# Sixteen column-tiled products in the output projection, expert weights loaded later, one loop of ScalarE written out

## What is computed

```python
q, k, v = heads(ln(x) @ Wq.T + bq), heads(ln(x) @ Wk.T + bk), heads(ln(x) @ Wv.T + bv)
out = softmax(q @ k.T / sqrt(8)) * head_mask @ v        # per head
x = x + merge(out) @ Wo.T + bo                          # the output projection
y = ln(x)
shared = gelu(y @ Wfc_s + bfc_s) @ Wproj_s + bproj_s
topk_p, topk_i = top_k(softmax(y @ Wr), 2)              # renormalised to gates
routed = sum over the 2 chosen e of gate[e] * (gelu(y @ Wfc[e] + bfc[e]) @ Wproj[e] + bproj[e])
x = x + shared + routed
```

## Time and profile before

| | us |
|---|---|
| time, median of 3 runs | 620.09 (620.05 to 621.78) |
| the profiled execution, its own time | 626.37 |
| its span, first to last instruction | 624.5 |
| outside of the span | 1.87 |

### The profile page before, as it was taken

One profiled execution on the slowest core, in us unless ns is written; L12 is line 12 of the kernel. 1 busy time (PEld: TensorE's weight loads), 2 busy tenths in 40 slices (PEclk: granted clock), 3 DMA queues, 4 the chain that ended last, 5 costly groups with the idle time before them and its releaser, 6 DMA issues. The chain is left out here.

```text
span 624.5 us, 21597 instructions
## 1 busy us (share of the span) xinstructions
PE 604.4 (97%) x8090; PEld 393.9 (63%) x8090; DVE 496.0 (79%) x1076; ACT 449.0 (72%) x971; POOL 279.3 (45%) x477
## 2 busy tenths in 40 slices
PE   6888899999999999999999999999999999999997
PEld 3443557665455555545555455457799999989966
DVE  7799789999899899899899889636466666666557
ACT  4976788888888888888878878884255555555551
POOL 6856520132542543542542632656545554545510
PEclk8998989999999999999999999999999999999999
DMA  6795954211312322223223221002222222222173
GB/s 172 214 306 175 268 155 112 66 53 43 95 50 63 83 55 66 74 54 77 64 57 80 59 58 43 20 27 67 62 64 66 64 67 60 67 59 68 47 264 149
DMA packets 43836, 57.63 MB, mean 92 GB/s; under 512 B 11130, under 2 KB 31482, under 8 KB 43754
## 3 DMA queue, kind: packets, MB, share of 16 engines
q1 hardware_dynamic: 39434, 47.59, 26.9%
q0 software_dynamic: 4320, 8.89, 4.3%
HBM read 35.76 MB, written 20.42 MB: 90 GB/s over the span
## 5 line engine op out<-in xcount | busy, mean ns | idle before, releaser
L979 DVE TENSOR_REDUCE mx<-ps 128x2 f32<-128x1024 f32 x256 | 306.5, 1214 | 32.0 <-PE ps L1400 27.3
L837 ACT ACTIVATE probs<-ps 128x512 f32<-128x512 f32 x512 | 292.8, 602 | 46.2 <-PE ps L1428 31.4
L1428 PE MATMUL ps<-q_op,k_op 128*32 128x512 bf16 x2048 | 201.9, 383 | 3.3 <-DMA q_op<-mxT 2.1
L1400 PE MATMUL ps<-k_op,q_op 96*32 96x512 bf16 x2048 | 160.4, 383 | 3.6 <-DVE mx L979 3.2
L1443 PE MATMUL ps<-probs,v_op 128*32 128x256 f32 x2048 | 158.5, 380 | 0.2 <-ACT probs L837 0.2
L895 ACT ACTIVATE probs<-ps,b_cur 128x128 f32<-128x128 f32 x284 | 80.9, 368 | 65.3 <-PE ps L1643 60.6
L711 POOL DMA_INDIRECT results<-rest,row_id x71 | 73.0, 1028 | 75.1 <-DVE rest L1282 58.0
L1400 PEld LDWEIGHTS ps<-k_op,q_op 96*32 96x32 bf16 x2048 | 56.9, 97 | 63.1 <-DVE mx L979 21.1
L1428 PEld LDWEIGHTS ps<-q_op,k_op 128*32 128x32 bf16 x2048 | 59.8, 96 | 57.7 <-ACT probs L837 10.0
L1443 PEld LDWEIGHTS ps<-probs,v_op 128*32 128x32 f32 x2048 | 66.1, 109 | 41.6 <-issue 1.4
L604 POOL DMA_INDIRECT slots<-route_sb,slot_u x64 | 63.5, 992 | 54.4 <-ACT probs L837 45.7
(11 more groups left out here) (176 smaller groups left out, 555.7 us busy)
## 6 DMA issues: line engine op xcount, KB each, us to landing
q_op<-q_scr SPq DMA_DIRECT2D x96, 96.0 KB
k_op<-k_scr SPq DMA_DIRECT2D x96, 96.0 KB
w_sb<-in_W SPq DMA_DIRECT2D x18, 256.0 KB, 4.6
probs<-slots SPq DMA_DIRECT2D x71, 64.5 KB
q_scr<-probs SPq DMA_DIRECT2D x8, 384.0 KB, 3.3
k_scr<-probs SPq DMA_DIRECT2D x8, 384.0 KB, 3.0
k_scr<-probs SPq DMA_DIRECT2D x8, 256.0 KB, 3.8
probs<-results SPq DMA_DIRECT2D x4, 512.0 KB, 6.2
```

Source lines behind the costliest of these rows:

```text
L837: nc.scalar.activation(probs[:, i, j, :], ps[:, BANK["key", b, hg, s], :], ACT.Exp, scale=float(D) ** -0.5).then_inc(s_exp, 1)
L979: nc.vector.reduce_max(mx[:, slot % 2, 2 * p:2 * p + 2], ps[:, bank:bank + 2, :], AX.X).then_inc(s_max, 1)
L1400: last = nc.tensor.matmul(ps[c, BK_A + a % 4, :], q_op[hg][0:SH, j, P * i + c.start:P * i + c.stop], k_op[hg][0:SH, j, :], start=True, sto ...
L1428: last = nc.tensor.matmul(ps[c, bank, :], k_op[hg][:, j, P * i + c.start:P * i + c.stop], q_op[hg][:, j, :], start=True, stop=True)
```

## The change

Three edits:

- `project_out` (new L1463) makes each of its four products of 128 rows of the output as four column-tiled ones with 32 rows each: sixteen, of the same K = 128 and the same 128 streamed columns, into the same places of PSUM. It holds for all 8 sequences, the last of which is projected between the `up`s.
- `load_experts` is split. The biases go out with group 1 of sequence 0 and `fill_slots` with group 2. The weights of one expert (512 KB) go out with each group of the sequences 1 and 2 and with the first group of sequence 3.
- ACT's loop over tiles 8 to 63 is written out, with constants in its waits.

```diff
--- before.py
+++ after.py
@@ -388,14 +388,15 @@
                 to = slots[E * REGION:E * REGION + E * TR, :].rearrange("(e p) c -> p e c", p=P)
                 sp.dma_start(to, y2s[1].rearrange("p n k c -> p (n k) c")).then_inc(s_fill, 16)
 
-            def load_experts(hg):
-
-                if hg == 0:
-                    sp.dma_start(b2_sb[:, :, :], b2.partition_broadcast(P)).then_inc(s_b2, 16)
-                    sp.dma_start(b1_sb[:, :, :], b1).then_inc(s_wffn, 16)
-                for e in range(hg, NE, HG):
-                    sp.dma_start(w1_sb[:, e, :], W1[:, e, :]).then_inc(s_wffn, 16)
-                    sp.dma_start(w2_sb[:, e, :, :], W2[:, e, :, :]).then_inc(s_wffn, 16)
+            def load_biases():
+
+                sp.dma_start(b2_sb[:, :, :], b2.partition_broadcast(P)).then_inc(s_b2, 16)
+                sp.dma_start(b1_sb[:, :, :], b1).then_inc(s_wffn, 16)
+
+            def load_expert(e):
+
+                sp.dma_start(w1_sb[:, e, :], W1[:, e, :]).then_inc(s_wffn, 16)
+                sp.dma_start(w2_sb[:, e, :, :], W2[:, e, :, :]).then_inc(s_wffn, 16)
 
             def feed(b):
                 first, last = isinstance(b, int) and b == 0, isinstance(b, int) and b == B - 1
@@ -408,10 +409,12 @@
                         load_shift(b, hg + 1)
                     elif not last:
                         load_shift(b + 1, 0)
-                    if first:
-                        load_experts(hg)
-                        if hg == 1:
-                            fill_slots()
+                    if first and hg == 1:
+                        load_biases()
+                    elif first and hg == 2:
+                        fill_slots()
+                    elif not first and (b - 1) * HG + hg < NE:
+                        load_expert((b - 1) * HG + hg)
 
             sequences(feed)
 
@@ -897,10 +900,7 @@
 
             for u in range(RING):
                 tile_gelus(u, u % TQ)
-            with act.Fori(1, TILES // RING) as it:
-                for u in range(RING):
-                    tile_gelus(it * RING + u, u % TQ)
-            for t in range(TILES // RING * RING, TILES):
+            for t in range(RING, TILES):
                 tile_gelus(t, t % TQ)
 
 
@@ -1459,7 +1459,9 @@
                 pe.wait_ge(s_o, b + 1)
                 bank = wait_for_bank("project", b) if b < B - 1 else BK_M
                 for i in range(NT):
-                    last = nc.tensor.matmul(ps[:, bank, C * i:C * (i + 1)], o_sb[:, P * i:P * (i + 1)], wo_sb[:, :], start=True, stop=True)
+                    for c in QUARTERS:
+                        last = nc.tensor.matmul(ps[c, bank, C * i:C * (i + 1)], o_sb[:, P * i + c.start:P * i + c.stop], wo_sb[:, :],
+                                                start=True, stop=True)
                 last.then_inc(s_ap, 1)
 
             def transpose_y(b):
```

## The result

Seven executions of the kernel after took 626.36 to 628.72 us, median 627.93. Beside the seven of the kernel before that belong to them (620.05 to 624.73, median 623.18; the first three are those shown ahead) the ratio is 1.007, 95% interval 1.0039 to 1.010. The forecast was 614.2 us, faster, with a range up to 618.8. The profiled execution took 628.69 us with a span of 626.9, against 626.37 and 624.5 before: it is 2.4 us longer, where the sum said 5.9 us shorter. So 8.3 us are to be found.

What follows compares the result with a forecast made beforehand. PE was taken to set the pace in the attention with next to no slack. From the 620.09 us median, -3.9 (weights), -2.1 (seven projections), +0.1 (eighth) and 0 (ACT's loop) gave 614.2 us, range 611.0 to 618.8.

Steps and rivals of the forecast that it cites:

- the sum: Whole kernel: -3.9 for later weights, -2.1 for seven projections, +0.1 for the eighth, -5.9 us in all.
- What bounds the kernel: Attention: PE sets the pace with next to no slack, 10.4 us of products per group of heads.
- Edit 1, -3.9: Sequence 0, shift rows issued at 69.92: later weights remove PE's stall behind queued transfers, -3.9 us (bounds 0 to -4.0).
- stall moves: Rival, sequences 1 to 3: groups now carrying weights stall PE, 3.9 us each, 625.9 us with three; chance 0.08.
- stall stays: Rival, sequence 0: the group load alone makes the shift rows late, only the projection's gain is left, 618.1 us; chance 0.12.
- Edit 2, 7 x 0.30: Seven projections in the attention: sixteen column-tiled products avoid the tiling switches, 0.30 us saved each, -2.1 us.
- The eighth, +0.1: Last projection, between whole-array products: it gets the tiling switches; entry hidden by a wait, exit costs 0.1 to 0.15 us.
- Edit 3, 0: Tile stage: ACT's loop ends lie inside time it would spend waiting for PE, so 0 (bounds -2.4 to +2.0 us).
- The signs: Even shift rows, no wait for them, full clock, 1.55 to 1.6 us around a projection, tile stage unchanged without new ACT waits.
- R2: Rival theory of the experiments: later weights delay something in sequences 1 to 3, taking the gain back, 1.000 or above; no chance given.

Runs made afterwards that it cites:

- e2: Kernel before with the projection's sixteen column-tiled products for four as the only edit; 1.0005 of the kernel before.
- q4: Kernel before with ACT's tile loop written out as the only edit; 1.0003 of the kernel before.
- g1: Kernel before, unchanged, run again for a second profile; no ratio given, it is the kernel before of its set.
- e1: Kernel before with only the later loads (weights, biases, fill), the projection as four products; 0.9972 of the kernel before.
- p4: The same kernel as e1, run once more in a later set; 0.9959 of the kernel before.
- g2: Kernel after, unchanged, run again; 1.0066 of the kernel before.
- q2: Kernel after with a POOL memset of 64 columns and a wait for it ahead of the first put of sequences 2 to 7; 1.006 of the kernel before.
- g4: Kernel after with sixteen products in sequences 0 to 2 alone, four in the others; 0.9977 of the kernel before.
- p2: Kernel after with a POOL memset of 192 columns between the waits and the first put of sequences 2 to 7; 0.9969 of the kernel before.
- e4: Kernel after with a POOL memset of 4 columns ahead of each sequence's first put; 0.9963 of the kernel before.
- q3: As q2, with the last projection as four products; 1.0016 of the kernel before.
- r2: As q3, with a memset of 256 columns in place of 64; 1.0029 of the kernel before.
- e3: Kernel before with a POOL memset of 4 columns ahead of each sequence's first put; 1.0012 of the kernel before.

## Why the prediction was wrong, point by point

**What bounds the kernel** held: PE sets the pace. Without held posts what the products saved came out of the distance from the first to the seventh projection in full.

**Edit 1, -3.9**: the mechanism was right, the size was read from one execution that had the stall at its largest. PE's wait for the shift rows in the second profile of before and in two others with the early weights (e2, q4):

```profile
77.35 0.40 PE L1428 MATMUL ps<-q_op,k_op 128*32 128x512 bf16 x4 [2.20 <-DMA q_op<-mxT]
```

```profile
75.44 0.40 PE L1428 MATMUL ps<-q_op,k_op 128*32 128x512 bf16 x4 [0.69 <-DMA q_op<-mxT]
```

```profile
75.61 0.40 PE L1425 MATMUL ps<-q_op,k_op 128*32 128x512 bf16 x4 [1.09 <-DMA q_op<-mxT]
```

In the eight profiles with early weights the distance of the shift rows' issues there was 14.4, 12.8, 11.7, 11.3, 10.9, 10.7, 10.5 and 10.5 us, where 10.4 is undisturbed: in the middle of them the stall is 0.7 us, not 3.9. The halved clock that the prediction counted into the 3.9 us varies with it. In the first profile 2.06 us of idle time were followed by 3.4 us at half the clock; in g1 an idle time of 2.20 us at the same place was followed by the full clock, and the distance is 1.5 us shorter. In the rows of g1 the busy times of PE, PEld, DVE, ACT and POOL follow the stretch and its length, and behind them the clock, 1.00 (0.50 and 0.69 in the earlier trace rows):

```profile
77.00:79.00 2.00, 1.65 (x32) 0.98 (x36) 0.76 (x1) 1.14 (x2) 2.00 (x2) 1.00 1.15 240
79.00:81.00 2.00, 2.00 (x44) 1.00 (x36) 1.85 (x3) 1.79 (x4) 2.00 (x3) 1.00 0.84 168
```

By the medians of many executions edit 1 gave -1.7 (e1) and -2.5 us (p4), intervals -2.9 to -0.4 and -3.9 to -1.0. The profiled execution stood 6.3 us above the median of the first runs, and the prediction carried that over unchanged with the words that the stall needs no profiler. It does not, but it varies; a profile far above the median is a warning that the priced pause may be one of its own. The rivals on weights (stall moves, stall stays) did not come.

**Edit 2, 7 x 0.30**: the products' own time is right to a few hundredths, -0.34 each. The step that failed is the sentence "ACT's copy of the result waits for PE there and moves forward with it". It held where posts are not held. Where they are, the copy moved back by a microsecond, PE came to wait for ACT (five waits that were not there), and from the first to the seventh projection the sixteen products take about 3 us more, where they take 2 less without held posts. No row ahead showed this place late, because the four products posted in time there, as they did in all 45 cases above; but the kernel before had waits on "remote" elsewhere, on one core with nobody remote, and I passed over them. From its waits between 434 and 444 us:

```profile
ACT probs L866 <- remote: 8.5, 1, 8.5
DVE x_sb L1214 <- remote: 2.3, 1, 2.3
```

**The eighth, +0.1**: it was costed "on a side where the last layer norm's chain does not wait". The chain waits for exactly this post: DVE's L1009 starts 0.1 us behind it. Held, it started 1.8 to 3.1 us late; not held, what comes with the fetch that PE's longer stream moved onto a put cost about 2. Two different mechanisms with nearly the same bill, and both were priced at nothing. In the kernel after with held posts both are at work: the fetch falls at 10.2 us behind the last projection, onto the last put of sequence 6 (10.0 to 10.9 us), `slot_u` waits 0.74 us for that put's landing, and PE 0.99 us for the first tile's rows (0.70 and 0.81 in g2, 0.40 and 1.32 in q2). How the 2.4 us divide between them no run says; g4, with the fetch alone, lost nothing at the tiles.

**Edit 3, 0**: right (1.0003; q4).

**The signs.** Every sign of being right that the prediction named came: the distances of about 10.4 us, no wait for the shift rows, the full clock, 1.54 us from `row_scores` to the `pv` behind the projection, and a tile stage of the same length without new waits of ACT. They looked at the priced places alone, none at the one who waits for the projection.

**The sum.** Not held: -2 (edit 1), -2.4 (seven), +2 (fetch), 0 is -2.4 us; measured -1.9 and -2.2 (p2, e4). Held: -2, +3 (the seven, their saving counted in) and +2.5 is +3.5 us; measured +4.1 (g2). These sums are put together afterwards from the profiles' stages, so their closeness proves little. None of the rivals was this; the slower one named a stall that did not move.

**What stays open**: why posts are held on some occasions and not on others, on the same chip too, and which ends are held, above all why the projection's post is always held beside a put with sixteen products and never with four. That the sixteen products would be free with their end clear of every put was not shown. Edit 1 alone, 0.9959 and 0.9972 where posts are not held, was not run where they are, so R2 is not excluded there for the sequences 1 to 3, in which the weights go out. A kernel that is faster than before on both occasions was not found with certainty: edit 1 with few sixteens (g4) is at 0.9977 held, and after with four products in the last projection is at 0.9936 not held, but at 1.0016 and 1.0029 held (q3 and r2, the same with a memset).

## What to carry to other kernels

A shorter operation is worth its saving only if the one who waits for it learns of its end; check the lag between the end of a producer and the start of an idle consumer at the places the change touches, and what the other engines start in that instant, a scatter by POOL above all. A list of signs should have one for each consumer of what is changed. Price a stall from more than one execution, and take a profiled time far above the median as a sign that its pauses may be large. Count the instructions that an edit adds to an engine's stream, since they shift every later fetch.

## What the runs showed of the hardware

- On some occasions completions of PE, ACT and DVE that fall beside an indirect transfer of POOL (0.96 to 1.03 us long, its record) are posted late: in g1 half of PE's held ones by over 0.6 us and one in ten by over 1.4, ACT's by 0.3 to 1.8, DVE's by 1.3 and more; the last projection's, where four such transfers follow each other, by 1.8 to 3.1 us. Of the completions of PE further than 1.6 us behind a transfer's start at most three of some 690 are. On other occasions profiles of nearly the same kernel (e1, e3), the first on a chip that held posts later, show about ten late posts in place of 280. The kernel before takes 607 us in the one and 623 us in the other on that chip.
- The post of the projection beside such a transfer was late in 39 of 39 cases with sixteen column-tiled products and in none of 45 with four on the whole array.
- One fetch of PE's instructions (16 KB) beside an indirect transfer goes with a landing about 0.5 us later: the reduction that waits for it starts 0.5 to 0.6 us later in e2, e4, p2 and g4.
- A memset of 64, 192 or 256 columns on POOL ahead of an indirect transfer moves its record by 0.03 us; the transfer's record starts 0.69 us behind the memset's start with each size.
- The same idle time of PE at the same place, 2.06 and 2.20 us, was followed by 3.4 us at half the clock in one execution and by the full clock in another.
